# Orders of ScalarE and VectorE by when inputs come, rows turned behind the route, control ahead of LoRA, results stored by SP

## What is computed

```
k[h]  = 2 Re( sum_n Cs[h,n] exp(dtA[h,n] * l) ),  l = 0..1023      (64 modes a head)
u     = x masked by the sequence's length
y     = causal convolution of u with k[h]  + D[h] * u, masked
x1    = x + y
base  = x1 @ W.T                                  (1024 x 1024)
logit = x1 @ Wr.T (8 experts) + 5 * onehot(language)
gates = softmax over the top 2 logits, scattered to 8 experts
lora  = sum_e gates[e] * (x1 @ A[e].T) @ B[e].T   (rank 16)
out   = x1 + base + 2 * lora
```

## Time and profile before

| | |
|---|---|
| median of 3 runs | 644.91 us (644.09 to 646.82) |
| profiled execution | 645.27 us, its span 643.5 us |
| TensorE clock granted, mean | 0.991 |
| TensorE busy | 619.5 us, 96% |
| VectorE busy | 524.1 us, 81% |
| ScalarE busy | 437.9 us, 68% |
| GpSimd busy | 34.7 us, 5% |
| chain that ended last | DVE 32%, PE 23%, issue 22%, ACT 16% |

### The profile page before, as it was taken

How to read it: one execution, slowest core, us unless ns; L and a number is a source line. 1 busy time by engine, 2 the same in 40 slices (tenths; PEclk the granted TensorE clock), 3 DMA queues, 4 the chain that set the end, 5 groups by cost and what they waited for, 6 DMA issues and landing times.

```text
span 643.5 us, 12483 instructions
## 1 busy us (share of the span) xinstructions
PE 619.5 (96%) x3439; PEld 592.7 (92%) x3439; DVE 524.1 (81%) x1560; ACT 437.9 (68%) x949; POOL 34.7 (5%) x61
## 2 busy tenths in 40 slices
PE   4798989999999999999999999999999999999997
PEld 4697989999999999999999999999999999999997
DVE  7887778888888888888888888888888888887741
ACT  5788687686676768667685867668576867764421
POOL 2241000000000000000000000000000000000000
PEclk9798999999999999999999999999999999999999
DMA  6531424443233444433334443232444432331212
GB/s 182 165 106 34 75 42 75 74 73 61 52 53 56 72 73 73 73 56 54 56 54 73 73 73 66 56 58 41 73 73 73 73 58 52 51 59 42 42 33 66
DMA packets 137856, 43.41 MB, mean 67 GB/s; under 512 B 127304, under 2 KB 132208, under 8 KB 137840
## 3 DMA queue, kind: packets, MB, share of 16 engines
q1 hardware_dynamic: 132960, 27.39, 25.6%
q10 hardware_dynamic: 4880, 15.83, 10.0%
HBM read 26.35 MB, written 16.85 MB: 67 GB/s over the span
## 4 chain that ended last, share of the span: by engine, by line
DVE 32%; PE 23%; issue 22%; ACT 16%; SPq 3%; ACTq 2%; DMA 1%; DVEq 1%
DVE state L970 11%; PE pmg L1313 11%; PE pc L1248 8%; ACT swapped L555 7%; DVE xt L1011 5%; ACT state L563 2%; DVE s_lo L999 2%; DVE zo_lo L922 2%; PE pmg L1300 1%; DVE gate L1044 1%; ACTq L606 1%; ACT t_hi L539 1%; ACT zo_hi L546 1%; ACT result L600 1%; DVE angle L787 1%
## 5 line engine op out<-in xcount | busy, mean ns | idle before, releaser
L1313 PE MATMUL pmg<-w_hi,y_hi 128*128 128x384 f32 (+1 forms) x768 | 263.2, 343 | 1.7 <-DVE y_lo L1017 1.7
L1313 PE MATMUL pmg<-w_hi,y_lo 128*128 128x384 f32 (+1 forms) x768 | 259.9, 338 | 0.0
L1313 PE MATMUL pmg<-w_lo,y_hi 128*128 128x384 f32 (+1 forms) x768 | 259.7, 338 | 0.0
L1313 PEld LDWEIGHTS pmg<-w_hi,y_hi 128*128 128x128 f32 x768 | 144.2, 188 | 2.7 <-issue 2.1
L1313 PEld LDWEIGHTS pmg<-w_hi,y_lo 128*128 128x128 f32 x768 | 144.3, 188 | 0.5
L1313 PEld LDWEIGHTS pmg<-w_lo,y_hi 128*128 128x128 f32 x768 | 144.2, 188 | 0.0
L555 ACT ACTIVATE swapped<-state 64x128 f32<-64x128 f32 x192 | 59.3, 309 | 66.3 <-DVE state L970 64.9
L970 DVE SCALAR_TENSOR_TENSOR state<-swapped,scan_tab,state 128x192 f32<-128x192 f32 (+1 forms) x240 | 73.7, 348 | 16.5 <-ACT swapped L555 12.1
L600 ACT ACTIVATE result<-pmg 128x384 f32<-128x384 f32 (+1 forms) x96 | 41.7, 449 | 39.4 <-PE pmg L1300 37.2
L1017 DVE TENSOR_TENSOR y_lo<-xt,y_hi 128x1024 fp32r<-128x1024 f32 x32 | 39.2, 1225 | 20.6 <-ACT y_hi L582 19.2
L970 DVE SCALAR_TENSOR_TENSOR state<-state,scan_tab 128x64 f32<-128x64 f32 x180 | 51.3, 327 | 3.1
(11 more groups left out here) (208 smaller groups left out, 1063.5 us busy)
## 6 DMA issues: line engine op xcount, KB each, us to landing
out<-result ACTq DMA_DIRECT2D x60, 256.0 KB, 4.3
rows<-in_x SPq DMA_DIRECT2D x224, 64.0 KB, 3.6
toe<-kpad SPq DMA_DIRECT2D x30, 128.0 KB, 4.8
rows<-in_x SPq DMA_DIRECT2D x8, 256.0 KB, 3.9
rows<-in_L_cond_W SPq DMA_DIRECT2D x3, 512.0 KB, 6.5
result<-in_L_cond_W SPq DMA_DIRECT2D x3, 512.0 KB, 6.4
w_rows<-in_L_cond_W SPq DMA_DIRECT2D x2, 512.0 KB, 4.8
result<-in_L_cond_A SPq DMA_DIRECT2D x1, 512.0 KB, 5.9
```

The costliest lines, as they stand in the source:

```text
L1313: ins = nc.tensor.matmul(pm[:, n, 0:o1 - o0], y[s][:, c, :], w[:, c, o0:o1], start=(c == 0 and y is y_hi and w is w_hi), stop=(c == CH - 1 ...
```

## The change

VectorE's step gets another order. The split that is ready first comes first, `k_col` and the other split go into `route` in place of `hold` copies (`behind_logits`, `behind_top`), `turn_rows` of pair i+2 stands behind the route of pair i (before, pair i+3 was turned at the step's end), `split_gated` stands behind the wait for the convolution in `merge`, and of a group's four Z2 tiles two are rotated in each step (`rotate_pair`, two of them by scalars from the new `second_tab`, which POOL stages). The scan's first add starts with the copied even states (`evens_ready`), before they are swapped.

ScalarE's step gets another order as well: the evacuation and `split_states` early, the Exp table load behind `split_states` in odd steps and the Sin load ahead of `waves` in even ones, `magnitudes` and `turn_powers` ahead of `split_turned`, the states copied ahead of `split_y`, and the two evacuations behind it. The swap reads `state` (SBUF) and not `v_psum`. TensorE runs the control ahead of LoRA, and LoRA after three chunks of the third bank. SP stores the results.

```diff
 def store_result(b, m):                      # SP, new; called in its step behind load_blocks
+    i, s = 2 * b + m, m % 2
+    sp.wait_ge(pm_free, 3 * i + 6)
+    for h in range(2):
+        sp.dma_start(bass.AP(out.tensor, (2 * i + h) * LEN, [[HEADS * LEN, SEQS], [1, LEN]]),
+                     result[s][h * SEQS:(h + 1) * SEQS, :]).then_inc(result_dma[s], 16)
@@ POOL
+            def stage_second(g):
+                vec.tensor_copy(second_tab[:, :], tab[:, CC_IM, bass.ds(g * DUO + 2, 2)]).then_inc(second_staged, 1)
+            stage_second(2)
             with pool.Fori(1, LOOPS) as b:
-                pool.wait_ge(z2_ready, b + 2)
+                pool.wait_ge(z2_turned, 2 * b - 1)
                 stage_gen(b + 2)
                 pool.wait_ge(scan, SCAN * (2 * b + 2))
                 stage_scan(b + 1)
+                pool.wait_ge(z2_turned, 2 * b)
+                stage_second(b + 2)
@@ ScalarE: copy_states
-                nc.scalar.activation(state[:, :, EVENS, :], v_psum[:, :, EVENS, :], ACT.Copy)
-                swap_state(i, slice(0, CARRIED - 1, 2), v_psum).then_inc(v_copied, 1)
+                nc.scalar.activation(state[:, :, EVENS, :], v_psum[:, :, EVENS, :], ACT.Copy).then_inc(evens_ready, 1)
+                act.wait_ge(evens_ready, i + 1)
+                swap_state(i, slice(0, CARRIED - 1, 2), state).then_inc(v_copied, 1)
@@ ScalarE: step
                 split_toe(b, m + 1)
-                if rows_left:
-                    split_ctr(b, m + 2)
-                    split_obs(b, m + 2)
                 evacuate(b, m - 1, 2)
                 if rows_left:
-                    split_turned(b, m + 2)
+                    if m == 1:
+                        split_obs(b, m + 2)
+                    split_ctr(b, m + 2)
+                split_states(b, m + 1)
+                if rows_left and m == 0:
+                    split_obs(b, m + 2)
+                if kernels and m == 1:
+                    nc.scalar.activation(warm[:, :], phase[:, 0:1], ACT.Exp)
                 ratios(b, m)
                 if kernels and m == 0:
                     act.wait_ge(gen_staged, b)
                     turns_of(None, True)
+                    magnitudes(None, True)
                 if kernels and m == 1:
                     swap_powers(b + 2)
-                store(b, m - 1)
+                    turn_powers(b + 2, True)
+                if rows_left:
+                    split_turned(b, m + 2)
                 split_gated(b, m)
                 if kernels and m == 0:
-                    magnitudes(None, True)
+                    nc.scalar.activation(warm[:, :], phase[:, 0:1], ACT.Sin)
                     waves(b + 2)
-                if kernels and m == 1:
-                    turn_powers(b + 2, True)
+                if rows_left:
+                    copy_states(b, m + 2)
+                split_y(b, m + 1)
                 for j in range(2):
                     evacuate(b, m, j)
-                split_y(b, m + 1)
                 if rows_left:
-                    copy_states(b, m + 2)
-                    if kernels and m == 0:
-                        nc.scalar.activation(warm[:, :], phase[:, 0:1], ACT.Exp)
                     for n in range(3):
                         swap_odd(b, m + 2, n)
-                    split_states(b, m + 2)
@@ VectorE: scan_states
-                dve.wait_ge(v_copied, i + 1)
+                dve.wait_ge(evens_ready, i + 1)
                 add(ODDS, state, slice(0, CARRIED - 1, 2), A_RE, into=v_psum)
                 dve.wait_ge(scan, start + 1)
+                dve.wait_ge(v_copied, i + 1)
@@ VectorE: step
+                toe_split = partial(split_toe, b, m + 1)
+                if rows_left:
+                    obs_split = partial(split_obs, b, m + 2)
+                    early, late = (obs_split, toe_split) if m else (toe_split, obs_split)
+                    early()
+                    low_ct(b, m + 2)
+                    if kernels and m == 1:
+                        powers(b + 2)
+                    route(b, m, partial(kernel_column, m + 2), late)
+                    turn_rows(b, m + 2)
+                else:
+                    route(b, m, behind_top=toe_split)
                 split_states(b, m + 1)
                 if rows_left:
                     split_rows(b, m + 2)
                 if kernels and m == 0:
                     angles(b + 2)
+                merge(b, m + 1, partial(split_gated, b, m))
+                if ahead and m == 0:
+                    dve.wait_ge(second_staged, b)
+                    rotate_pair(b + 1, 1, [second_tab[:, h:h + 1] for h in range(2)])
+                if ahead and m == 1:
+                    rotate_pair(b + 2, 0, [gen_scalar(CC_IM, None, h, True) for h in range(2)])
+                if rows_left:
+                    dve.wait_ge(scan_staged, b + m // 2 + 1)
+                    scanning = scan_states(b, m + 2)
+                    next(scanning)
                 split_y(b, m + 1)
+                if rows_left:
+                    for _ in scanning:
                         pass
-                if ahead:
-                    turn_rows(b, m + 3)
@@ TensorE: step
                 if rows_left:
-                    turn_powers(b, m + 2)
+                    turn_powers(b, m + 2, halves_turned=2 * b + m - 1)
                 wait_y(b, m)
                 project(b, m, 0)
                 project(b, m, 1)
-                turn_gates(b, m, 2 * b + m + 3 if rows_left else PAIRS)
+                turn_gates(b, m, 2 * b + m + 3 if rows_left else PAIRS, 2 * b + m + 3 if rows_left else None)
                 convolve(b, m + 1)
-                add_loras(b, m)
                 if rows_left:
                     control(b, m + 2, alone=True)
-                project(b, m, 2)
+                project(b, m, 2, 0, 3)
+                add_loras(b, m)
+                project(b, m, 2, 3, 8)
                 add_lora(BANK_ORDER[2])
```

More of the change, by code:

```diff
@@ L2 @@
 from contextlib import ExitStack
+from functools import partial
 import concourse.bass as bass
@@ L125, in cond_resid_kernel @@
         gen_tab = sb("gen_tab", [P, 4, DUO])
+        second_tab = sb("second_tab", [P, 2])
         scan_tab = sb("scan_tab", [P, 4, DUO])
@@ L230, in cond_resid_kernel @@
         z_half, z2_half, row_full = sem("z_half"), sem("z2_half"), sem("row_full")
+        z2_turned = sem("z2_turned")
+        second_staged, evens_ready = sem("second_staged"), sem("evens_ready")
         z_swapped, z2_ready = sem("z_swapped"), sem("z2_ready")
@@ L356, in _, with store_result @@
             load_toe(0, 3)
+            def store_result(b, m):
+                i, s = 2 * b + m, m % 2
[3 more added lines that the diff above has]
+                                 result[s][h * SEQS:(h + 1) * SEQS, :]).then_inc(result_dma[s], 16)
             def step(b, m, rows_left=True):
@@ L361, in step @@
                     load_blocks(b, m + 4)
+                store_result(b, m)
                 store_kernel(b, m + 3)
@@ L371, in _ @@
             step(LOOPS, 0, rows_left=False)
+            store_result(LOOPS, 1)
+            store_result(LOOPS + 1, 0)
             def store_last(j, heads):
@@ L750, in _ @@
             ratios(LOOPS + 1, 1)
-            store(LOOPS + 1, 0)
             split_gated(LOOPS + 1, 1)
@@ L933, in split_ctr, with low_ct, kernel_column, rotate_pair @@
                                   ).then_inc(clo_ready, 1)
+            def low_ct(b, m):
+                dve.wait_ge(chi_ready, 2 * b + m + 1)
+                vec.tensor_tensor(c_lo[:, :, :], ct_psum, c_hi[:, :, :].bitcast(F32), ALU.subtract
+                                  ).then_inc(clo_ready, 1)
+            def kernel_column(m):
+                vec.reduce_sum(k_col[m % 2][:, :], ct_psum[:, :, 0:MODES], axis=mybir.AxisListType.X).then_inc(k_ready, 1)
+            def rotate_pair(g, j, scalars):
+                dve.wait_ge(z_swapped, g + 1)
+                for h in (2 * j, 2 * j + 1):
+                    ins = vec.scalar_tensor_tensor(out=Z2[:, h, :], in0=z_swap[:, h, :], scalar=scalars[h - 2 * j],
+                                                   in1=Z2[:, h, :], op0=ALU.mult, op1=ALU.add)
+                ins.then_inc(z2_turned, 1)
             def rotate_powers(g, staged):
@@ L1003, in hold, with merge @@
                 vec.tensor_copy(held[:, :], lang_f[:, :])
-            def merge(b, m):
+            def merge(b, m, behind_conv=hold):
                 i, s = 2 * b + m, m % 2
@@ L1008, in merge @@
                 dve.wait_ge(conv_done, i + 1)
-                hold()
+                behind_conv()
                 for h in range(2):
@@ L1018, in split_y, with route @@
                                   ).then_inc(ylo_ready, 1)
-            def route(b, m):
+            def route(b, m, behind_logits=hold, behind_top=hold):
                 i = 2 * b + m
@@ L1026, in route @@
                 dve.wait_ge(router, base + 1)
-                hold()
+                behind_logits()
```

(36 more changed lines are left out.)

1 line of the change is left out of this document (removed).

## The result

The median went from 644.5 us (4 runs, 643.49 to 646.82) to 636.76 us (4 runs, 635.94 to 638.81): a ratio of 0.988, 95% interval 0.9844 to 0.9916. The profiled execution took 635.94 us, its span 633.7 (before 645.27 and 643.5). Forecast was 636.6.

A forecast was written before the change was run, and what follows sets the result against it. TensorE bounds the kernel, busy 442.61 of 444.50 us, so only its waits can be regained: 6.5 (odd steps) + 1.0 (step (1,1)) + 0.8 (step (1,0)) = 8.3, giving 637.0 profiled, 636.6 median; range 635.0 to 642.5.

The forecast's parts named there:

- odd steps: Main loop: gate transpose's wait for gated goes, 18.79 to 18.25 us; twelve odd steps by 0.54 give 6.5 us.
- step (1,1): Second step of the loop: from 19.24 to the 18.25 floor, a gain of 1.0 us.
- `logits`: Start of VectorE's route in odd steps: 4.6 us into the step instead of 6.57, set by gate_done, idle time before.
- the scan ended: VectorE's scan: ends 2.25 us into the next step, against 2.98 before.
- Step (1,0): First loop step, 20.79 us: gate hole of 0.58 goes and 0.25 of y_lo's 1.96; together 0.8.
- The spare at u_lo: Ahead of TensorE's control: u_lo ends at 10.97 us into the step, control due at 11.42; smallest spare, 0.2 to 0.3.
- R3: Rival: u_lo loses the race each step; beyond 0.55 late the kernel loses, 0.8 late gives 652 us; chance 0.08.
- R1: Rival: u_lo or s_lo partly late, each 0.1 beyond the spare costing 2.8 us: 639.4 or 642.2; chance 0.20.
- R2: Rival: Exp table load holds ScalarE 2.58 us, half_sum 0.9 late, nothing gained, 645 us; chance 0.05.
- R4: Rival: scan ends 2 us later than worked out, gate wait stays, 645 us; chance 0.05.
- VectorE's lateness: Odd route comes 2 us late because scan, rows turned (1.30), three splits, kernel column and Z stand ahead.
- ScalarE's new order: ScalarE's reordered step: all costed at nothing; if u_hi's cover of 0.4 is gone, one for one.

The follow-up runs named there:

- e4: Changed kernel plus one scratch VectorE subtraction (some 0.6 us) between the route and the turning of the rows; 652.49 us, ratio 1.012.
- e2: Changed kernel with the rows turned at the step's end again, as before; 636.40 us.
- e3: Changed kernel with TensorE running LoRA, control and the whole third bank as before, gt_lo behind u_lo; 645.38 us, ratio 1.000.
- e11: Changed kernel with ScalarE copying the states last, behind both evacuations and y_hi, which also moved behind the evacuations; 713.99 us in one run.
- e9: e3 with gt_lo directly behind s_lo, ahead of u_lo; 637.67 us, ratio 0.988.
- e1: Kernel before with the rows turned behind the route, gt_lo ahead of u_lo, and pair 4's rows no longer turned in the prologue; 667.31 us, ratio 1.035.
- e5: Kernel before with only VectorE's edit: kernel column and t_lo inside the route, without ScalarE's new order; 650.43 us, ratio 1.008.
- e7: Kernel before with only the result stores moved from ScalarE's queue to SP's; 644.84 us, ratio 0.999.
- e8: e1 with ScalarE making t_hi, c_hi and zo_hi ahead of s_hi; 638.74 us, ratio 0.991.
- e12: Kernel before with ScalarE making s_hi behind t_hi, c_hi, zo_hi and the evacuation, rows unmoved; 640.63 us, ratio 0.993.
- e13: e12 plus VectorE's kernel column and t_lo (odd steps) inside the route; 637.75 us, ratio 0.989.

## Why the prediction came out

**The mechanism and the main terms were right.** Only odd steps had a hole; twelve of them gave 6.52 us (forecast 6.5), step (1,1) 0.98 (19.24 to 18.26; forecast 1.0). `logits` started at 4.7 (forecast 4.6) with idle time before it, the scan ended at S+2.4 in both steps (2.25).

**Step (1,0) was mis-sized:** 20.79 to 20.60, 0.2 instead of 0.8. The gate hole of 0.58 went. But y_lo gained 0.05, not 0.25: it waits 0.27 for y_hi, since ScalarE came later against TensorE there. And 0.42 was lost anew, which the sum had left out. Its route still starts late (92.27, with z waiting 0.41 for zo_hi, which ScalarE makes behind s_hi in even steps). So s_lo ends at 97.63 and costs TensorE 0.14, and u_lo ends at 99.08:

```profile
97.85 1.23 DVE L923 TENSOR_TENSOR u_lo<-xt,u_hi 128x1024 fp32r<-128x1024 f32 x1 [0.22 <-ACT u_hi L552]
```

```profile
99.28 0.44 PE L1293 MATMUL px<-u_hi,c_hi 128*128 128x448 f32 x1
```

The control, due at 99.08, starts at 99.28, and its first matmul takes some 0.08 longer: 0.28.

**The spare at u_lo was mis-sized:** forecast 0.2 to 0.3, it is 0.1. u_lo ended at S+11.16 and 11.09, not 10.97 (gate_done 0.1 later, and u_lo starts 0.11 behind the end of u_hi), and by e4 TensorE starts 0.20 behind u_lo's end, not 0.13: 11.42 - 0.20 - 11.16 = 0.06 in even, 0.13 in odd steps. In step (14,0), which stands outside the loop, u_lo ends at the same 11.16 and 0.15 is lost: the control starts at 573.93, 0.35 behind u_lo and not 0.20. In e4 it is 0.35 there too (589.59 to 589.94); why it is more outside the loop is not shown. R3 put the point from which the kernel loses at u_lo 0.55 us later; by e4, 0.60 costs 15.7 us over 28 steps (0.56 each), so that it loses from 7.7/28 + 0.05, some 0.3 us.

**The rest of the difference is the prologue.** The span fell by 9.8 us: 7.54 between step (1,0) and step (14,1), and 2.28 ahead of step (1,0), which begins at 85.58 instead of 87.86. The orders there are the same up to pair 2's merge, but the source of the swap and the earlier first add hold for the prologue's pairs too. In the other traces with the changed prologue that step begins at 86.2 (e2, e3, e4, e11) and 87.5 (e9), in those with the old one at 86.8 to 90.5 (e1, e5, e7, e8, e12, e13), and from 50 to 60 us the mean granted clock was 0.83 in the trace before and 1.00 in the one after, though 0.83 in e2 as well, which is at 86.2. The spread is as large as the difference; whether a microsecond of it belongs to the change stays open. The medians, 7.74 apart, don't need it. The steps gave 0.8 less than forecast, and the medians of the kernel before alone lie between 644.5 and 645.8; that the median after came within 0.2 of the forecast is in part luck.

**The rivals.** R1 came true in step (1,0), and a little in (14,0) and (14,1). R2 did not: in the odd step after,

```profile
329.03 1.28 ACT L742 ACT_TABLE_LOAD   x1
330.32 0.20 ACT L742 ACTIVATE warm<-phase 128x1 f32<-128x1 f32 x1
330.48 0.30 ACT L607 ACTIVATE ratio<-top 128x1 f32<-128x1 f32 x1
```

the load takes 1.28, its first user starts 1.29 behind the load, the ratio 0.16 behind that, and half_sum waits for nothing. The 1.38 us of drain that the Trainium skill has in "ScalarE: Activation LUTs", section "What ACT_TABLE_LOAD costs", is not seen here. R3 and R4 did not come.

**What the prediction did not see is where the gain came from.** It put VectorE's lateness down to the work ahead of its route, the rows first of all, and costed ScalarE's new order at nothing. e2 shows that the rows' move gives nothing, e1 that alone it costs 22 us, e12 and e13 that s_hi behind t_hi, c_hi and zo_hi, with k_col and t_lo inside the route, is enough. Whether the changed kernel, with the scan's end 0.6 us earlier, still needs that order was not tried, and the Z2 tiles rotated two a step were in no run by themselves. In the earlier trace rows t_lo starts at 317.54, 0.13 behind the rows: it was waiting for t_hi, and the rows hid that wait. Taking away that cover alone uncovered 1.35 us in e1. The control ahead of LoRA earns little by the earlier scan (0.11 in odd steps, by e9); for the rest it pays for the late gt_lo, and it leaves u_lo 0.1 of spare.

## What to carry to other kernels

When two engines alternate, look for the instruction that waits for the latest input and stands ahead of ones whose inputs are long there; moving it back is worth more than moving the work that hides the wait. Before crediting a part of a reorder, run it alone and on top of the others. Here the rows' move cost 22 us alone (e1), and twelve pairs of e8 are within 0.2 us of e12, which has ScalarE's order without it. k_col and t_lo inside the route cost 5 alone (e5) and gave 2.1 in twelve pairs on top of that order (e13 against e12). A place where a matmul waits costs its lateness, the start behind the late input and a longer first matmul, here 0.2 to 0.3 us together in the loop. A spare of 0.1 us is soon gone.

## What the runs showed of the hardware

In e11 TensorE stood for 1.9 us ahead of the matmul at 298.28. It began again at the old pace, and from 299.81 to 303.08 its matmuls came 0.33 us apart instead of 0.175. That is the lower of its two levels, 1.2 GHz; the mean granted clock of the stretch was 0.68, and in the next one it was back at 0.97. So in four even steps (21.97 instead of 20.43 us) a wait of 1.9 us cost some 1.5 more; the same wait in the other steps did not. The 0.54 us waits of the kernel before left the clock at 1.00.

TensorE started 0.13 to 0.15 us behind the end of `gated` (303.24 to 303.37 in the kernel before), of gt_lo (304.78 to 304.92 in e3) and of s_lo (301.05 to 301.19 in e9), 0.20 behind u_lo in the loop, and 0.35 behind it in step (14,0). The first 448-column matmul behind such a wait was recorded with 0.44 us instead of 0.36.
